# A delta-rule decoder layer on one core: values and Wo in two fp16 parts, decay factors made inside the keys-only steps

## What is computed

```python
q, k, v = [causal_conv_silu(x @ W, w, b) for ...]   # 4 taps; 16 heads, q and k 128 wide, v 256 wide
q, k = l2norm(q), l2norm(k)
alpha, beta = sigmoid(x @ Wa), sigmoid(x @ Wb)       # one of each per token and head
def step(state, (qt, kt, vt, at, bt)):               # over the 64 tokens
    state = state * at
    err = vt - einsum('bhkv,bhk->bhv', state, kt)
    state = state + bt * einsum('bhk,bhv->bhkv', kt, err)
    return state, einsum('bhkv,bhk->bhv', state, qt)
out = outs.reshape(b, t, 32 * 128) @ Wo
x = x + out(layernorm(x))
x = x + xattn(layernorm(x), ctx, ctx)
x = x + ffn(layernorm(x))                            # w1, w2 -> w + (clip(round(w / mean|w|), -1, 1) - w)
```

## Time and profile before

| | |
|---|---|
| median of 3 runs | 2775.72 us (2772.84 to 2776.93) |
| the profiled execution | 2775.03 us, of which 2773.2 us are the span of the trace |
| PE busy | 2374.7 us, 86% of the span |
| PEld busy | 1479.4 us, 53% |
| DVE busy | 1707.5 us, 62% |
| ACT busy | 1275.4 us, 46% |
| POOL busy | 1129.4 us, 41% |
| granted PE clock, mean | 0.90 of full speed |
| chain that ended last | PE 65%, issue 10%, DVE 8%, POOL 7%, SPq 6% |

### The profile page before, as it was taken

One profiled execution on the slowest core, in us unless ns is written; L12 is line 12 of the kernel. 1 busy time (PEld: TensorE's weight loads), 2 busy tenths in 40 slices (PEclk: granted clock), 3 DMA queues, 4 the chain that ended last, 5 costly groups with the idle time before them and its releaser, 6 DMA issues.

```text
span 2773.2 us, 60971 instructions
## 1 busy us (share of the span) xinstructions
PE 2374.7 (86%) x21440; PEld 1479.4 (53%) x21440; DVE 1707.5 (62%) x2652; ACT 1275.4 (46%) x2383; POOL 1129.4 (41%) x1495
## 2 busy tenths in 40 slices
PE   2454559999999999999999999999888578888887
PEld 2221226665665665666666566666555355565555
DVE  6664547676666676666666667666333256566654
ACT  2232325555555555555555555555333234444443
POOL 1294465636537355274463653735700101111112
PEclk9978889999999999999999999999998756767777
DMA  7233232333333324323233333332321010010100
GB/s 260 88 151 129 58 70 81 78 81 90 76 81 89 82 68 98 85 66 93 81 78 80 88 74 79 94 82 67 81 45 35 26 39 25 28 29 29 29 13 16
DMA packets 438381, 204.09 MB, mean 74 GB/s; under 512 B 371088, under 2 KB 392336, under 8 KB 435600
## 3 DMA queue, kind: packets, MB, share of 16 engines
q1 hardware_dynamic: 438032, 199.71, 27.0%
HBM read 127.28 MB, written 72.35 MB: 72 GB/s over the span
## 4 chain that ended last, share of the span: by engine, by line
PE 65%; issue 10%; DVE 8%; POOL 7%; SPq 6%; DMA 3%; ACT 2%; POOLq 0%; DVEq 0%; ACTq 0%
PE PS L1157 19%; PE PS L1170 13%; PE PS L1232 7%; POOL SCR L545 4%; PE PS L1339 3%; PE PS L1248 3%; PE PS L1352 3%; PE PS L1307 3%; PE PS L1205 2%; PE PS L1324 2%; PE PS L1218 2%; DVE Y L945 2%; PE PS L1363 2%; DMA SCR<-PGD 2%; PE PS L1189 1%
## 5 line engine op out<-in xcount | busy, mean ns | idle before, releaser
L945 DVE SCALAR_TENSOR_TENSOR Y<-PS,CW,Y 128x504 f32<-128x504 f32 (+2 forms) x1536 | 1124.7, 732 | 678.9 <-ACT Y L712 646.9
L712 ACT ACTIVATE Y<-PS,CW 128x512 f32<-128x512 f32 x512 | 398.4, 778 | 629.1 <-PE PS L1157 629.1
L1170 PE MATMUL PS<-WO,XN 128*128 128x256 f32 x2048 | 504.2, 391 | 45.3 <-issue 44.3
L1170 PEld LDWEIGHTS PS<-WO,XN 128*128 128x128 f32 x2048 | 395.5, 194 | 129.5 <-issue 50.3
L594 POOL TENSOR_TENSOR SQ<-KQ 128x512 f32<-128x512 f32 x128 | 133.3, 1042 | 521.5 <-PE PS L1196 502.0
L1157 PE MATMUL PS<-XK,WH 128*128 128x512 f16 x1024 | 313.9, 389 | 22.0 <-DMA XK<-XHD 21.2
L1157 PE MATMUL PS<-XV,WH 128*128 128x512 f16 x1024 | 314.3, 389 | 1.9 <-DMA XV<-XHD 1.9
L737 ACT ACTIVATE XN<-PS,KN 128x256 f32<-128x256 f32 x512 | 215.0, 471 | 169.8 <-PE PS L1170 169.8
L580 POOL TENSOR_TENSOR SCR<-SCR 128x31 f32<-128x31 f32 (+15 forms) x496 | 267.5, 539 | 38.9
L577 POOL TENSOR_TENSOR SCR<-SCR 128x31 f32<-128x31 f32 (+15 forms) x496 | 242.3, 489 | 42.2 <-issue 9.2
L1232 PE MATMUL PS<-XN,M 64*64 64x256 f32 x2048 | 249.7, 383 | 1.0 <-issue 1.0
(11 more groups left out here) (128 smaller groups left out, 3000.7 us busy)
## 6 DMA issues: line engine op xcount, KB each, us to landing
PGD<-SCR SPq DMA_DIRECT2D x128, 256.0 KB, 2.1
SCR<-PGD SPq DMA_DIRECT2D x128, 256.0 KB, 3.0
EQD<-SCR SPq DMA_DIRECT2D x8, 2048.0 KB, 6.3
SCR<-EQD SPq DMA_DIRECT2D x128, 128.0 KB, 2.5
SCR<-QND SPq DMA_DIRECT2D x128, 128.0 KB, 3.2
XP<-in_x SPq DMA_DIRECT2D x16, 512.0 KB, 4.6
SCR<-in_wall SPq DMA_DIRECT2D x8, 1024.0 KB, 6.3
SCR<-PGD SPq DMA_DIRECT2D x64, 128.0 KB, 3.3
```

What stands on the lines that cost most here:

```text
L712: A_.activation(Y[:, b, :], PJ[b][:, :], ACT.Identity, scale=CW[:, h[1] % NH, cw0 + 3:cw0 + 4], bias=CW[:, h[1] % NH, cw0 + 4:cw0 + 5]).th ...
L945: V_.scalar_tensor_tensor(yv[:, :, m:T], pv[:, :, 0:T - m], CW[:, h[1] % NH, cw0 + 3 - m:cw0 + 4 - m], yv[:, :, m:T], ALU.mult, ALU.add).t ...
L1170: ins = mm(VWB[:, E * i:E * i + E], V[:, n, P * a:P * a + P], WO[:, 2 * (w[1] % NH) + n, :], start=(n == 0), stop=(n == 1))
```

## The change

- **Values and Wo in two fp16 parts.** WO (fp32) is replaced by WOS with a high and a low part, scaled by WS = 64, made from four chunks in SCR like the other weights. ACT takes SiLU twice for each value bank, once into VHL as fp16 and once in place as fp32, and DVE subtracts (low_values): 256 new instructions on ACT and 256 on DVE. values makes 12 fp16 matmuls a half, where it made 4 of fp32. state_product divides by WS in the same instruction.
- **Decays in the keys-only steps.** Four units of the 32 are made before the first step, 28 in the steps (AT_STEP: one in each of the first 8, two in each of the next 10). The rows (DVE) are made one step ahead; two pairs of banks, 0 and 1 or 5 and 6, take turns. The causal mask is added by PE (IDH by MASKN, which holds 0 or -500) ahead of the exponential, so that POOL's 64 instructions are gone. Each unit is stored by itself, to 256-byte pieces of EQD.
- **Ternary weights** are made in halves in steps 3, 5, 15 and 17; w2 is loaded a second time.
- **Order.** On PE, values moves behind the projections, and outputs behind the projection of bank 2. On ACT, tap(v, 0) stands ahead of values(w, 0), and values(w, 1) behind silu_v(v, 0). On DVE the convolution of bank 3 moves to the start of the next step.
- **Gates** take 24 matmuls of 32 columns a group in place of 48 of 16, and gates_in is done one pass later.

```diff
-        WO = sb("WO", [P, 2 * NH, E])
+        WOS = sb("WOS", [P, 2, 2 * NH, E], F16)
@@ sync @@
-            for g in range(G):
-                s = g % 2
-                sp.wait_ge(S["masked"], at(8 * g + 8))
-                sp.dma_start(EQD[g].rearrange("p h x -> p (h x)"), scr(4096 * s, 4096)).then_inc(S[f"st_eq{s}"], 16)
+            def store_eq(n):
+                g, p, s = n // NP, n % NP, n % 2
+                sp.wait_ge(S["dec_exp"], at(n + 1))
+                sp.dma_start(EQD[g].rearrange("p h (a t) -> p h a t", t=T)[:, :, p, :], EQB[s]).then_inc(S[f"st_eq{s}"], 16)
@@ gpsimd @@
-            for g in range(G):
-                for p in range(NP):
-                    for n in range(2):
-                        pool.wait_ge(S["dec_exp"], at(8 * g + 2 * p + n + 1))
-                        eq = EQB[g % 2][:, 8 * n:8 * n + 8, p, :]
-                        nc.gpsimd.tensor_tensor(eq, eq, CST[:, C_MQ:C_MQ + 64][:, None, :].broadcast_to([P, 8, T]), ALU.mult).then_inc(S["masked"], 1)
@@ scalar @@
+            def exponents(n):
+                s = n % 2
+                act.wait_ge(S["dec_mm"], at(n + 1))
+                if n >= 2:
+                    act.wait_ge(S[f"st_eq{s}"], at(16 * (n // 2)))
+                for i in range(2):
+                    ins = A_.activation(EQB[s][:, 8 * i:8 * i + 8, :], DECB[s][i][:, :].rearrange("p (h t) -> p h t", h=8), ACT.Exp)
+                ins.then_inc(S["dec_exp"], 1)
             def silu_v(v, b):
                 act.wait_ge(S[f"conv{b}"], heads(v, 3, 3))
                 act.wait_ge(S["vw_mm"], heads(v, 2))
-                A_.activation(V[:, b, :], Y[:, b, :], ACT.Silu).then_inc(S[f"silu{b}"], 1)
+                A_.activation(VHL[:, 0, b, :], Y[:, b, :], ACT.Silu)
+                A_.activation(Y[:, b, :], Y[:, b, :], ACT.Silu).then_inc(S[f"silu{b}"], 1)
@@ scalar, step @@
                 if exists(kp):
                     silu_kq(kp, 2)
+                if exists(v):
+                    tap(v, 0)
                 if exists(w):
                     values(w, 0)
-                if exists(v):
-                    tap(v, 0)
...
                     tap(v, 1)
                     silu_v(v, 0)
+                if exists(w):
+                    values(w, 1)
                 if exists(k):
                     tap(k, 2)
@@ vector, step @@
+                if exists(back(k)):
+                    for m in (1, 2, 3):
+                        conv(back(k), 3, m)
...
+            def low_values(v, b):
+                dve.wait_ge(S[f"silu{b}"], heads(v, 1, 1))
+                dve.wait_ge(S["vw_mm"], heads(v, 2))
+                V_.tensor_tensor(VHL[:, 1, b, :], Y[:, b, :], VHL[:, 0, b, :], ALU.subtract).then_inc(S["vl_done"], 1)
@@ tensor @@
             def values(w, half):
                 if half == 0:
-                    pe.wait_ge(S["silu0"], heads(w, 1, 1))
-                    pe.wait_ge(S["silu1"], heads(w, 1, 1))
+                    pe.wait_ge(S["vl_done"], heads(w, 2, 2))
                 pe.wait_ge(S["vw_ev"], heads(w, 2, half))
                 for i in range(2):
                     a = 2 * half + i
+                    t = 0
                     for n in range(2):
-                        ins = mm(VWB[:, E * i:E * i + E], V[:, n, P * a:P * a + P], WO[:, 2 * (w[1] % NH) + n, :], start=(n == 0), stop=(n == 1))
+                        for vk, wk in ((0, 0), (0, 1), (1, 0)):
+                            ins = mm(VWB[:, E * i:E * i + E], VHL[:, vk, n, P * a:P * a + P], WOS[:, wk, 2 * (w[1] % NH) + n, :],
+                                     start=(t == 0), stop=(t == 5))
+                            t += 1
```

More of the change, by code:

```diff
@@ L427, in keep, with stored_eq @@
                 sp.dma_start(X1D[ds(g, 1)].rearrange("o p n e -> (o p) n e"), XP[:, 0]).then_inc(S["st_x1"], 16)
+            def stored_eq(units):
+                for s in range(2):
+                    sp.wait_ge(S[f"st_eq{s}"], at(8 * units))
             sp.wait_ge(S["zero_e"], at(2))
+            stored_eq(NP)
             sp.dma_start(XK[:, :, :], XHD[0]).then_inc(S["ld_xk"], 16)
@@ L686, in _ @@
                     act.wait_ge(S["tr_done"], at(2 * g + c + 1))
-                    A_.activation(XB[:, s, c, 0:GT], PJ[2 * s + c][:, :], ACT.Copy).then_inc(S["xh_done"], 1)
+                    A_.activation(XB[:, s, c, :], PJ[2 * s + c][:, :], ACT.Copy).then_inc(S["xh_done"], 1)
                 split(g)
+            for n in range(8, 12):
+                split(n)
             act.wait_ge(S["z_done"], at(G))
@@ L775, in step @@
                     silu_v(v, 1)
+                units = units_of(v, k)
+                for n in units[:1]:
+                    exponents(n)
                 if exists(k):
                     tap(k, 3)
+                for n in units[1:]:
+                    exponents(n)
             schedule(act, step)
@@ L1267, in step @@
                 if exists(w):
-                    outputs(w)
+                    values(w, 1)
                 if exists(v):
@@ L1272, in step @@
                     project(k, 2, XK, "ld_xk")
+                for n in units[:1]:
+                    decays(n)
+                if exists(w):
+                    outputs(w)
                 if exists(back(k)):
```

240 lines of the change are left out of this document (140 added, 100 removed).

## The result

The changed kernel takes 2601.1 us (median of 4 runs, 2598.91 to 2605.14), against 2775.68 before in the same comparison: a ratio of 0.9378, 95% interval 0.9362 to 0.9394. That is 174.6 us less; 155 were forecast, and the range of 2578 to 2685 holds the time. The profiled execution has a span of 2596.8 us, 176.4 less than before.

A forecast was written before the change was run, and what follows sets the result against it. PE was taken to bound the full steps (98% busy). Setup -9, decays -120, keys-only steps +40, full steps -44 and steps without a k -22 sum to -155 from 2775.03, thus 2620 us; 80% range 2578 to 2685.

The forecast's parts named there:

- Setup and decays: Before the first step: setup -9 us (DVE's wait for gates goes), decays -120 (POOL's masking chain goes).
- Full steps: Full steps: shorter values products on PE, step 13.2 to 13.25 us from 13.75; net -44, bounds -90 to 0.
- a stall before the outputs: Full steps: PE idles some 0.3 us before the outputs, for ACT's scaling behind the SiLU pair.
- batch boundaries: Full steps: at 14 boundaries more ACT and DVE work between lanes and outputs, 0.7 us each: +10.
- tight estimate of 12.92: Full steps: two halves of the values save 0.83 us, and PE alone would need 12.92 a step.
- Rival (1): Full steps: no stall before the outputs, PE packed at 12.92 us a step; kernel 2585 us; chance 12%.
- Steps without a k: 19 steps of 12.9 us: 11.7 in the mean, 10.4 where the clock stays; -22, bounds -45 to +10.
- Keys-only steps: Keys-only steps: DVE's rows and ternary halves lengthen the loop, PE and ACT hidden; +40 us, bounds +25 to +70.
- Rival (2): Front gains less: setup bound by DMA, late stores holding back ACT, or slow rows; +15 to +60, 2660 us; 16%.
- The rule on table loads: Keys-only steps: the skill's 1283 ns load plus about 1380 drain would make 18 steps some 28 us longer, 2648.
- rival 4: low_values blocked by POOL on the shared SBUF port, 0.3 to 0.6 us more each; kernel 2650 us; chance 6%.
- The slower case: Full steps: idle before the outputs grows to about 1.9 us, clock falls to 0.88; kernel 2800 us; chance 3%.

The follow-up runs named there:

- same-pass gates: Changed kernel with gates_in back in the pass where it stood before (unit g-1 in pass g): 2613.55 us.
- scaling-first kernel: Changed kernel with ACT's values(w, 1) ahead of silu_v(v, 0): 2571.21 us, ratio 0.9255.
- fp16 kernel: Changed kernel with values, outputs and scalings at their old places on PE and ACT, fp16 parts kept: 2771.19 us, ratio 0.9969.

## Why the prediction was right, and where it wasn't

**Setup and decays.** -9.9 and -118.2 against -9 and -120. The four units with their store and the load of XK cost 23.4, where 22 were summed. But POOL was less of the cause than its 99.64 us in the earlier trace rows make it: with all 32 units ahead of the steps and no POOL the stretch is still 98.9 us (92.3 to 191.2), so most of the 118 is work moved, and comes back in the next stage. The same-pass gates show that the wait taken out of the earlier trace rows was real: 11.3 us for the later copy, where 16 were summed for it and for half as many matmuls, whose own part no run shows. What is late next was named wrongly: DVE waits there for the load of x (9.5 us), not for the weights' DMA.

**Full steps.** -57.9 against -44. The mechanism was as told: PE is the bound, a stall before the outputs eats part of the gain, and the batch boundaries give some back (the excess over the regular step is 30 us before and 38 after; +10 was forecast). The mis-sized term is the stall, 0.15 in place of 0.3. The tight estimate of 12.92 for PE without a stall is what the scaling-first kernel reached, and its terms hold. A product takes 0.109, as the earlier trace rows had it: inside a half of the values the starts are 109 ns apart, and dropping 8 saved 0.87. That a half takes 1.40 and not the 1.31 of the sum comes from 0.09 us more behind its last product, where 32*32 work follows. The second half before had the same 0.09 (1.82 from 1213.28 to 1215.10, where the first took 1.73). There are three such changes from 128*128 products to smaller ones in a step before and three after, so they drop out of the difference; the forecast didn't count them. Rival (1) was thus not the changed kernel, but one swap of two lines away from it.

**What carried the gain** was not seen: the forecast priced the new order as a cost only (the stall). With the fp16 parts and the old order there is no gain in the full steps at all, 14.45 against 13.75. The prediction never worked out the chain over the second SiLU and low_values for the old place of the values, and so missed that the fp16 parts need a place further from their preparation. The old order isn't hopeless for them: with the low part earlier on DVE its step is 13.58.

**Steps without a k.** -42.3 against -22; the step that failed is "the gap remains and the clock has fallen with it". The gap did remain (1.55 us), and the clock did not fall: 0.99 over the stage. The step of 10.47 is the 10.4 that the forecast had "where the clock stays". The 11.68 that it called regular was the rarer kind before, and fourteen steps of 13.37 are 24 us of clock, which the change gave back. The fp32 values in the new order show 1.00, the fp16 values in the old order 0.89, so it is the order and not the products that kept it. In the old order the idle time stands in one piece right ahead of the values, 3.07 us in the fp16 kernel and 1.87 before, and the values behind it run slow:

```profile
2067.45 2.64 PE L1247 MATMUL PS<-WOS,XN 128*128 128x256 f16 x12 [3.07 <-DVE XN L1017]
```

2.43 us to the next start, against 1.40 at 2071.74. What makes the chip grant less after a gap of 1.87 and not after one of 1.55 stays open, and so does why four of the eighteen steps before kept the full clock with the same 1.87; no run varied the gap alone.

**Keys-only steps.** +53.6 against +40. With all units ahead of the steps the stage is 187.4, which is 15.0 over before without a unit in it (the ternary halves, forecast at 11, are among that); the 28 units are the other 38.6. Of these, +33 for rows was too much: taking the rows out gave 14.6, since DVE is only the bound in the steps with one unit. PE, which the forecast called hidden, takes the step to 8.5 where there are two. The term that was missing is SP's queue: the stores stand ahead of the spill and of the lanes' loads, and putting them last gave 14.9. Rival (2) had late stores only as something that holds back ACT, which happened once, for 5.0 us. The table loads are hidden, as it said. So the first full step came at 341.7, behind the 327 to 335 that were named. The plain steps with one unit took 7.6 to 7.7 (7.8 were named), those that also make ternary weights up to 9.7, and those with two 9.0, as named.

**The rule on table loads.** The loads take 1.28 us, and the next instruction starts 0.01 later, in the changed kernel as in the earlier trace rows. Taking 34 of them away made no step with two units shorter. The Trainium skill, ScalarE: Activation LUTs, What ACT_TABLE_LOAD costs, has a second part of about 1380 ns for each switch; no row here shows it. (The forecast gave no working for its 28 us by that rule; the 35 loads in the steps at 1380 ns would be 48 us of ACT's time, an estimate from that figure of the Trainium skill.)

```profile
273.31 1.28 ACT L764 ACT_TABLE_LOAD   x1
274.60 0.63 ACT L764 ACTIVATE KQ<-Y 128x512 f32<-128x512 f32 x1
```

**low_values beside POOL** (rival 4). 256 of them, the median as good as the fastest, 13.4 us over that in all. Of the 148 that ran with POOL busy beside them nearly throughout, 31 took over 0.9 us and the others no longer than alone. It costs nothing that a step shows.

```profile
L1017 DVE TENSOR_TENSOR XN<-Y,XN x256: 677/681/2082, 347.3 to 2009.4; 128x512 f16<-128x512 f32 x128
```

(Columns after the count: shortest, median and longest in ns, then the first and last start.) **The slower case** did not occur: the clock is 1.00 in the full steps with a gap of 0.15.

## What to carry to other kernels

When an instruction is made of several shorter ones with a longer preparation, work out the chain from the preparation to its place in the old order too: here fp16 parts in the old order lost 0.7 us a step (with one move on DVE they won 0.2), and the same parts one projection later won 0.6. On an in-order engine, of two instructions that the same event releases, the one that another engine waits for goes first; that swap alone was worth 30 us here. And a store that waits for its data belongs at the end of its queue's step, behind everything that others wait for, as long as its buffer isn't needed before it lands: that was worth 15 us here, with ACT's waits for the landing up from 5.0 to 14.6.

## What the runs showed of the hardware

A DVE comparison of 1024 fp32 elements from and to SBUF takes 0.75 us by itself and 1.53 with POOL's square beside it, while low_values (fp32 and fp16 in) hardly changes; so making an engine that is not the bound earlier can cost time on another. Products of fp16 with 256 columns start 0.109 us apart at full clock, and dropping 8 of 24 saved that much each; behind the last 128*128 product, fp16 or fp32, another 0.09 us pass where work in 32*32 or 64*64 tiles follows. An issue of a 0.5 MB store in 256-byte pieces took 0.56 us in the median, but up to 5.0 where two came together, and the issue behind it 2.6 where it takes 0.36 in the kernel before.
